# A graph-attention kernel: q rows in two PSUM banks per batch, q in a rounded and a rest part, tile sums per pair

## The chip, the cores and the metric

One core of a Trainium2 chip runs the kernel. It has TensorE (matmuls into PSUM), VectorE, ScalarE, GpSimd (which here issues the gathers by row index) and SyncE (which issues the other DMAs), and 16 DMA engines. The metric is device microseconds of one execution, lower is better.

## The reference

One layer of graph attention over 6250 nodes and 100000 edges, with edges sorted by destination, C = 256 channels in H = 8 heads of 32, all in float32:

```python
q, k, v = x @ Wq.T + bq, x @ Wk.T + bk, x @ Wv.T + bv       # each [6250, 8, 32]
score = clip(einsum("ehd,ehd->eh", q[dst], k[src]) / sqrt(32), -10, 10)
alpha = exp(score - max over the edges of a destination), divided by its sum
wv = segment_sum(alpha * v[src], dst)                       # [6250, 256]
y = x + wv @ Wp.T + bp
y = y + gelu(layernorm(y) @ W1.T + b1) @ W2.T + b2          # hidden 1024
out = layernorm(x + y)
```

## The kernel before

**Rows of k and v.** A first phase (to about 82 us) projects x into k and v for 25 units of 256 nodes with f32r matmuls on parts (a rounded part and a rest, `split_matmul`, L834), adds biases on VectorE and stores rows of k and v side by side in DRAM (`kv_rows`, 2 KB a row). The q rows of the first two units (`EARLY_Q`) are made there too; those of the other 24 are made one unit a turn later (`project_q` on TensorE, `copy_q` L1183 on ScalarE, `store_q_unit` on SyncE) and lie in `q_rows`, 1 KB a row.

**Edges.** The main phase walks over the edges in 196 batches of 4 tiles of 128 edges. Two batches are a pair, eight a turn; the index of a batch within the turn is i. As edges are sorted by destination, the 8 tiles of a pair need few q rows: SyncE loads four windows of 32 rows of q per pair into `qwin`, one per 32 partitions (`load_q_windows`, L597), two pairs ahead. For batch n:

- GpSimd gathers the k and v rows of the edges' sources, four indirect DMAs of 128 rows (L394), into one of 8 slots of `kv`. It may overwrite a slot when `ev` of batch n-8 is done (`s_ev`). A few tiles (one a turn) are instead projected from x by TensorE and copied by ScalarE.
- ScalarE makes the transposed one-hots `onehotT` (L1145, L1150), VectorE the upright ones `onehot` (L1550), per pair.
- TensorE multiplies one-hots with window rows into `quad`, four PSUM banks, 256 of each bank's 512 columns for one tile (`q_rows`, L895). Since the four banks hold one batch only, `q_rows(n+1)` waits for product n (`s_prod`).
- VectorE: `prod` = k times q rows (L1564), `score` = reduce over 32 (L1571), clip (L1578).
- ScalarE: exponent, once into PSUM bank 5 and once into `ev` (L1159, L1160).
- VectorE: `ev` = v times exponent (L1584). 
- TensorE: sums of the tiles into bank 4, each tile's nodes in a window of 32 partitions (`sums`, L904). The two batches of a pair accumulate.
- Per pair: ScalarE copies bank 4 (`stage`, L1168), TensorE merges the windows (`merge`, L884), ScalarE copies the merged sums into `acc_sb` (`copy_sums`, L1174), SyncE stores them (`store_sums`, L633). The next pair's sums write the same bank and wait for that copy (`s_accc`).

**Nodes.** Interleaved by hand, `node_steps(turn, i)` on each engine works on a unit of 256 nodes whose sums are complete: divide, transpose, project (L427), residual (L433), layer norm (VectorE root steps, L491 to L503), the feed-forward layers (`ffn1` L455 with ScalarE's bias L463, gelu, `ffn2` L475) and the output.

**Order.** Each engine has its program order written out in its own `edges` function, and waits on semaphores only. Before the change, iteration n of the four engines is:

```
TensorE: q_rows(n+1), merge of the pair two back (even n), node steps, sums(n-2)
VectorE: clip(n-1), product(n), onehots (even n), weight(n-2), node steps, scores(n)
ScalarE: exponent(n-1), copy_sums (even n), node steps, stage (odd n), transposed one-hots (even n)
GpSimd:  wait for ev of batch n-8, four gathers
```

`exists(...)` guards the ends. With i = 5 the node steps of TensorE stand behind the sums. `early_q` in the change is a view of `ev` that the first phase uses. There is a second, general path for inputs that the windows don't fit; it isn't run with these inputs.

## Time and profile before

| | us |
|---|---|
| median of 3 runs | 1517.91 |
| lowest and highest | 1514.08, 1532.04 |
| the profiled execution's own time | 1529.23 |
| its span, first to last instruction | 1527.4 |

The profile is one execution. Its page lists busy time by engine, the groups of instructions by line, DMA issues and the chain that ended last. Busy time of TensorE is the union of its matmuls, whose ends are modelled; a record of TensorE says when a matmul started, not when its signal arrived. An f32 matmul appears as two records, an f32r one as one. "x8" in a timeline row means that eight records follow each other without a gap. The bracket at a row's end is the idle time of that engine before it and what ended it; "remote" stands where the view finds no instruction that ended the wait, "issue" where the wait ended with no semaphore seen. The mean granted TensorE clock of this execution is 0.850 of full speed.

### The profile page before, as it was taken

How to read it: one execution, taken by the hardware profiler on the slowest of the kernel's cores; microseconds unless marked ns; L12 is line 12 of the kernel's file. 1: busy time of each engine (PE TensorE's matmuls, PEld its weight loads, DVE VectorE, ACT ScalarE, POOL GpSimd, SP SyncE). 2: the span in 40 equal slices, each digit the busy share in tenths (PEclk: the TensorE clock that was granted, in tenths of full speed). 3: DMA queues.
4: the chain of work that ended last, by engine and by line, in shares of the span. 5: the costliest groups of instructions: out<-in, count | busy, mean ns of one | idle time of the engine just before them, and what ended most of it. 6: DMA issues, size and time to landing. Idle time of an engine off the chain costs nothing.

```text
span 1527.4 us, 25002 instructions
## 1 busy us (share of the span) xinstructions
PE 1155.0 (76%) x6166; PEld 702.7 (46%) x6166; DVE 948.5 (62%) x1542; ACT 661.5 (43%) x1906; POOL 750.8 (49%) x800
## 2 busy tenths in 40 slices
PE   8946758768778588777678778677877876878887
PEld 6812325435444344444445444344444444545466
DVE  6816665666656565666666567576576665665673
ACT  2212225345445345345445435444545444534543
POOL 3664554545645544544555555545455545554300
PEclk9966868988978888979889888889788788898799
DMA  9975765655756656666666666756666656666510
GB/s 296 356 232 161 225 208 177 212 172 180 227 157 187 205 173 192 192 183 192 207 181 195 209 177 204 217 166 205 203 184 203 196 168 200 196 201 182 167 52 23
DMA packets 155028, 292.71 MB, mean 192 GB/s; under 512 B 32215, under 2 KB 92469, under 8 KB 154934
## 3 DMA queue, kind: packets, MB, share of 16 engines
q0 software_dynamic: 61536, 200.85, 43.6%
q1 hardware_dynamic: 93398, 90.90, 19.1%
q14 instruction: 72, 0.59, 0.1%
q8 instruction: 22, 0.36, 0.1%
HBM read 257.31 MB, written 34.34 MB: 191 GB/s over the span
## 4 chain that ended last, share of the span: by engine, by line
PE 32%; another core or an unknown queue 25%; issue 18%; DVE 18%; ACT 5%; DVEq 1%; ACTq 0%; DMA 0%; SPq 0%
DVE score L1571 7%; DVE ev L1584 6%; PE bank L475 5%; PE quad L834 4%; PE bank L455 4%; PE quad L895 4%; PE bank L904 4%; PE bank L427 2%; PE bank L917 2%; DVE prod L1564 2%; PE bank L930 1%; PE bank L884 1%; PE bank L421 1%; PE quad L455 1%
## 5 line engine op out<-in xcount | busy, mean ns | idle before, releaser
L394 POOL DMA_INDIRECT kv<-kv_rows,src_sb x750 | 713.7, 952 | 652.1 <-issue 326.4
L1564 DVE TENSOR_TENSOR prod<-kv,quad 128x1024 f32<-128x1024 f32 x196 | 239.3, 1221 | 426.3 <-remote 324.5
L904 PE MATMUL bank<-ev,onehot 128*32 128x264 f32 x1568 | 151.8, 451 | 160.7 <-ACT acc_sb L1174 101.4
L455 PE MATMUL bank<-hT,w_sb 128*128 128x256 f32 x736 | 219.2, 450 | 41.2 <-ACT hid L463 30.0
L1584 DVE TENSOR_TENSOR ev<-kv,bank 128x1024 f32<-128x1024 f32 x196 | 238.0, 1214 | 0.5 <-ACT ev L1160 0.5
L1571 DVE TENSOR_REDUCE score<-prod 128x32 f32<-128x1024 f32 x196 | 237.7, 1213 | 0.8
L895 PE MATMUL quad<-qwin,onehotT 32*128 32x256 f32 x1568 | 158.3, 476 | 79.1 <-issue 40.1
L455 PEld LDWEIGHTS bank<-hT,w_sb 128*128 128x128 f32 x736 | 162.8, 227 | 89.8 <-issue 45.4
L475 PE MATMUL bank<-w_sb,hid 128*128 128x256 f32 x736 | 190.9, 412 | 2.0 <-issue 2.0
L475 PEld LDWEIGHTS bank<-w_sb,hid 128*128 128x128 f32 x736 | 149.5, 208 | 32.0 <-issue 9.7
L1174 ACT ACTIVATE acc_sb<-bank 128x264 f32<-128x264 f32 x98 | 38.1, 389 | 290.7 <-remote 219.8
L463 ACT ACTIVATE hid<-bank,b_sb 128x256 f32<-128x256 f32 x184 | 77.1, 471 | 177.2 <-PE bank L455 76.0
L895 PEld LDWEIGHTS quad<-qwin,onehotT 32*128 32x128 f32 x1568 | 69.2, 205 | 181.5 <-issue 131.3
L904 PEld LDWEIGHTS bank<-ev,onehot 128*32 128x32 f32 x1568 | 35.5, 115 | 232.9 <-issue 206.5
L884 PE MATMUL bank<-staged,place 128*128 128x264 f32 x196 | 77.4, 480 | 54.6 <-ACT staged L1168 27.7
L930 PE MATMUL bank<-wqkv_in,xgT 128*128 128x512 f32 x120 | 80.7, 800 | 6.4 <-issue 6.1
L1159 ACT ACTIVATE bank<-clipped 128x32 f32<-128x32 f32 x196 | 38.4, 196 | 108.1 <-issue 75.9
L1168 ACT ACTIVATE staged<-bank 128x264 f32<-128x264 f32 x98 | 37.9, 387 | 84.6 <-remote 47.5
L884 PEld LDWEIGHTS bank<-staged,place 128*128 128x128 f32 x196 | 31.7, 203 | 92.2 <-issue 52.6
L421 PE MATMUL bank<-bias_rows,one_rows 2*128 2x512 f32 (+1 forms) x130 | 66.7, 513 | 8.9 <-issue 4.1
L427 PE MATMUL bank<-wp_sb,wvT 128*128 128x256 f32 x200 | 68.5, 502 | 0.0
L834 PE MATMUL quad<-wqkv_sb,xT_parts 128*128 128x512 f32 x288 | 67.2, 395 | 0.0
(148 smaller groups left out, 1297.7 us busy)
## 6 DMA issues: line engine op xcount, KB each, us to landing
dst_rows<-edge_dstT SPq DMA_DIRECT2D x50, 256.0 KB
qwin<-q_rows SPq DMA_DIRECT2D x392, 32.0 KB
kv_rows<-kv_out SPq DMA_DIRECT2D x24, 512.0 KB
kv<-kv_rows,src_sb POOLq DMA_INDIRECT x750
agg_rows<-acc_sb SPq DMA_DIRECT2D x98, 82.5 KB
xT_sb<-xT SPq DMA_DIRECT2D x25, 256.0 KB
xq_sb<-xT SPq DMA_DIRECT2D x25, 256.0 KB
agg_in<-agg_rows SPq DMA_DIRECT2D x24, 264.0 KB
```

The costliest lines, as they stand in the source:

```text
L394: return nc.gpsimd.indirect_dma_start(out=rows, out_offset=None, in_=kv_dram, in_offset=bass.IndirectOffsetOnAxis(ap=index, axis=0))
L427: last = nc.tensor.matmul(bank6[:, a * C:(a + 1) * C], wvT[:, (a * KC + k) * P:(a * KC + k + 1) * P], wp_sb[:, k * C:(k + 1) * C], start=F ...
L455: last = nc.tensor.matmul(bank[:, j * SB:(j + 1) * SB], w1_sb[:, k * HIDDEN + f * P:k * HIDDEN + (f + 1) * P], hT[:, k], start=(k == 0), s ...
L475: last = nc.tensor.matmul(bank[:, a * C:(a + 1) * C], hid[:, f, a * P:(a + 1) * P], w2_sb[:, f * C:(f + 1) * C], start=False, stop=(a == 1 ...
L834: last = nc.tensor.matmul(rows, lhsT, rhs, start=(n == 0), stop=(n == len(passes) - 1))
L884: nc.tensor.matmul(bank4[:, 0:ACC], place[:, slot % 2], staged[:, slot % 2], start=True, stop=True)\
L895: last = nc.tensor.matmul(quad[:, i, 0:C], onehotT[rows, slot // 2, cols], qwin[rows, slot // 2], start=True, stop=True)
L904: last = nc.tensor.matmul(bank4[WIN * i:WIN * (i + 1), 0:ACC], onehot[:, slot // 2, TILES * (slot % 2) + i, :], ev[:, slot % 4, i], start= ...
L930: last = nc.tensor.matmul(bank[:], columns[:, j], wqkv_in[:, j, C:3 * C], start=False, stop=(j == KC - 1))
L1564: nc.vector.tensor_tensor(prod[:, slot % 2].rearrange("p (i c) -> p i c", c=C), kv[:, slot, :, 0:C], quad[:, :, 0:C], ALU.mult).then_inc(s ...
L1571: nc.vector.tensor_reduce(score[:, slot % 2], prod[:, slot % 2].rearrange("p (h d) -> p h d", d=HD), AX.X, ALU.add).then_inc(s_score, 1)
L1584: nc.vector.tensor_tensor(ev[:, slot % 4, :, 0:C].rearrange("p i (h d) -> p i h d", d=HD), kv[:, slot, :, C:2 * C].rearrange("p i (h d) -> ...
```

## The change

- `q_rows` in DRAM has rows of 2 KB: the q row rounded to f32r, and the rest (q minus the rounded part). ScalarE's copy writes the rounded part, a new subtraction on VectorE the rest: `q_low` once a turn at i = 3, and one per early unit in the first phase (where the unrounded q is kept in `early_q`). Stores of q units become two DMAs. `qwin` and `onehotT` are f32r, `qwin` has both parts.
- `q_rows(n)` writes two whole banks: tiles 2i and 2i+1 of a pair share window i and bank i, so batch n uses banks 0 and 1 (even) or 2 and 3 (odd). Each tile takes two f32r matmuls that accumulate, rounded part and rest: eight matmuls of 256 columns, two windows at a time. It waits for product n-2, and TensorE's iteration n issues `q_rows(n+2)`. `q_rows(1)` moves into the opening.
- `sums` runs once per pair, in odd iterations, for all eight tiles; `s_part` counts pairs.
- `acc_sb` and `prod` lose half of their buffers (4 to 2, 2 to 1); the SBUF goes to `qwin`.
- The tiles of a pair are taken in their natural order; the tables of the host follow.

The diff, cut to its core ("..." marks what is left out: the general path, waits that count 32 instead of 16, the check's tables):

```diff
-    q_dram = nc.dram_tensor("q_rows", [Q_UNITS * SB, C], f32).ap()
+    q_dram = nc.dram_tensor("q_rows", [Q_UNITS * SB, 2 * C], f32).ap()
...
-        q_next = sb("q_next", [P, 2, C])
+        q_next = sb("q_next", [P, 2, 2, C], f32r)
...
-        onehotT = sb("onehotT", [P, 4, 2 * P])
+        onehotT = sb("onehotT", [P, 4, 2 * P], f32r)
         onehot = sb("onehot", [P, 4, PAIR_TILES, WIN])
-        qwin = sb("qwin", [P, 4, C])
+        qwin = sb("qwin", [P, 4, 2, C], f32r)
         ev = sb("ev", [P, 4, TILES, ACC])
-        acc_sb = sb("acc_sb", [P, 4, ACC])
+        acc_sb = sb("acc_sb", [P, 2, ACC])
...
-        prod = sb("prod", [P, 2, TILES * C])
+        prod = sb("prod", [P, TILES * C])
...
+        early_q = ev[:].rearrange("p a i n -> p (a i n)")[:, 0:EARLY_Q * 6 * C].rearrange("p (u t n) -> p u t n", u=EARLY_Q, t=3)
...
-                if u < EARLY_Q:
-                    sp.wait_ge(s_qb, u + 1)
-                    sp.dma_start(q_dram[u * SB:(u + 1) * SB, :].rearrange("(a p) n -> p a n", p=P), q_out[:, u])\
-                        .then_inc(s_qst, 16)
+                for e in range(EARLY_Q):
+                    if u == min(e + 2, UNITS - 1):
+                        sp.wait_ge(s_qlo, e + 1)
+                        for t in range(2):
+                            sp.dma_start(q_unit_rows(slice(e * SB, (e + 1) * SB))[:, t], early_q[:, e, t].rearrange("p (a n) -> p a n", n=C))\
+                                .then_inc(s_qst, 16)
...
-                    sp.dma_start(qwin[WIN * i:WIN * (i + 1), slot], q_dram[bass.ds(base + WINDOW_STARTS[i], WIN), :])\
-                        .then_inc(s_qwin[slot], 16)
+                    sp.dma_start(qwin[WIN * i:WIN * (i + 1), slot].rearrange("p t n -> p (t n)").bitcast(f32),
+                                 q_dram[bass.ds(base + WINDOW_STARTS[i], WIN), :]).then_inc(s_qwin[slot], 16)
...
             def store_q_unit(turn):
-                sp.wait_ge(f_qb, turn + 1)
+                sp.wait_ge(f_ql, turn + 1)
                 sp.sem_inc(s_gate_sp, 1)
-                sp.dma_start(q_dram[bass.ds((turn + EARLY_Q) * SB, SB), :].rearrange("(a p) n -> p a n", p=P), q_next[:])\
-                    .then_inc(f_qst, 16)
+                for t in range(2):
+                    sp.dma_start(q_unit_rows(bass.ds((turn + EARLY_Q) * SB, SB))[:, t], q_next[:, t].bitcast(f32))\
+                        .then_inc(f_qst, 16)
...
             def q_rows(n, slot, p, uses):
                 pe.wait_ge(s_qwin[slot // 2], 64 * uses)
                 pe.wait_ge(s_ohT, p + 1)
-                if exists(n - 1, BATCHES):
-                    pe.wait_ge(s_prod, n)
-                cols = slice(slot % 2 * P, (slot % 2 + 1) * P)
-                for i in range(TILES):
-                    rows = slice(WIN * i, WIN * (i + 1))
-                    last = nc.tensor.matmul(quad[:, i, 0:C], onehotT[rows, slot // 2, cols], qwin[rows, slot // 2],
-                                            start=True, stop=True)
+                if exists(n - 2, BATCHES):
+                    pe.wait_ge(s_prod, n - 1)
+                for j in range(2):
+                    for part in range(2):
+                        for i in (slot % 2 * 2, slot % 2 * 2 + 1):
+                            rows = slice(WIN * i, WIN * (i + 1))
+                            last = nc.tensor.matmul(quad[:, i, j * C:(j + 1) * C],
+                                                    onehotT[rows, slot // 2, j * P:(j + 1) * P],
+                                                    qwin[rows, slot // 2, part], start=(part == 0), stop=(part == 1))
                 last.then_inc(s_qe, 1)
 
-            def sums(n, slot, p):
-                pe.wait_ge(s_ev, n + 1)
-                if slot % 2 == 0 and exists(p - 1, PAIRS):
+            def sums(p, slot):
+                pe.wait_ge(s_ev, 2 * p + 2)
+                if exists(p - 1, PAIRS):
                     pe.wait_ge(s_accc, p)
-                for i in range(TILES):
-                    last = nc.tensor.matmul(bank4[WIN * i:WIN * (i + 1), 0:ACC],
-                                            onehot[:, slot // 2, TILES * (slot % 2) + i, :], ev[:, slot % 4, i],
-                                            start=(slot % 2 == 0 and (i > 0 or not exists(p - 1, PAIRS))),
-                                            stop=(slot % 2 == 1), skip_group_check=(i == 0))
+                for j in range(2):
+                    for i in range(TILES):
+                        tile = 2 * i + j
+                        last = nc.tensor.matmul(bank4[WIN * i:WIN * (i + 1), 0:ACC], onehot[:, slot, tile, :],
+                                                ev[:, (2 * slot + tile // TILES) % 4, tile % TILES],
+                                                start=(j == 0 and (i > 0 or not exists(p - 1, PAIRS))),
+                                                stop=(j == 1), skip_group_check=(i == 0))
                 last.then_inc(s_part, 1)
...
                 project_x(2, xgT)
+                q_rows(1, 1, 0, 1)
...
-                    pe.wait_ge(f_qb, s + 2)
+                    pe.wait_ge(f_ql, s + 2)
...
-                    if exists(n + 1, BATCHES):
-                        q_rows(n + 1, (i + 1) % SLOTS, 4 * turn + (i + 1) // 2, turn + (i + 1) // SLOTS + 1)
+                    if exists(n + 2, BATCHES):
+                        q_rows(n + 2, (i + 2) % SLOTS, 4 * turn + (i + 2) // 2, turn + (i + 2) // SLOTS + 1)
                     if i % 2 == 0 and exists(4 * turn + i // 2 - 2, PAIRS):
                         merge(4 * turn + i // 2 - 2, (i // 2 + 2) % 4)
                     if i != 5:
                         node_steps(turn, i)
-                    if exists(n - 2, BATCHES):
-                        sums(n - 2, (i - 2) % SLOTS, 4 * turn + (i - 2) // 2)
+                    if i % 2 == 1 and exists(4 * turn + i // 2 - 1, PAIRS):
+                        sums(4 * turn + i // 2 - 1, (i // 2 + 3) % 4)
...
+                for e in range(EARLY_Q):
+                    if u == min(e + 2, UNITS - 1):
+                        act.wait_ge(s_qb, e + 1)
+                        nc.scalar.activation(early_q[:, e, 0].bitcast(f32r), early_q[:, e, 2], ACT.Copy).then_inc(s_qhi, 1)
...
-            def exponent(n, slot):
+            def exponent(n, slot, p):
                 act.wait_ge(s_clip, n + 1)
                 if exists(n - 1, BATCHES):
                     act.wait_ge(s_ev, n)
                 if exists(n - 4, BATCHES):
-                    act.wait_ge(s_part, n - 3)
+                    act.wait_ge(s_part, p - 1)
                 first = EX_COL + slot % 2 * TILES * H
                 nc.scalar.activation(bank5[:, first:first + TILES * H], clipped[:, slot % 2], ACT.Exp, scale=SCALE)
                 nc.scalar.activation(ev[:, slot % 4, :, C:ACC],
...
                                      ACT.Exp, scale=SCALE).then_inc(s_exp, 1)
 
             def stage(p, slot):
-                act.wait_ge(s_part, 2 * p + 2)
+                act.wait_ge(s_part, p + 1)
                 if exists(p - 2, PAIRS):
                     act.wait_ge(s_mrg, p - 1)
                 nc.scalar.activation(staged[:, slot % 2], bank4[:, 0:ACC], ACT.Copy).then_inc(s_stc, 1)
 
             def copy_sums(p, slot):
                 act.wait_ge(s_mrg, p + 1)
-                if exists(p - 4, PAIRS):
-                    act.wait_ge(s_aggst, 16 * (p - 3))
-                nc.scalar.activation(acc_sb[:, slot], bank4[:, 0:ACC], ACT.Copy).then_inc(s_accc, 1)
+                if exists(p - 2, PAIRS):
+                    act.wait_ge(s_aggst, 16 * (p - 1))
+                nc.scalar.activation(acc_sb[:, slot % 2], bank4[:, 0:ACC], ACT.Copy).then_inc(s_accc, 1)
...
             def copy_q(turn):
                 act.wait_ge(f_qm, turn + 1)
                 if exists(turn - 1, Q_UNITS - EARLY_Q):
-                    act.wait_ge(f_qst, 16 * turn)
-                nc.scalar.activation(q_next[:].rearrange("p a c -> p (a c)"), bank6[:], ACT.Copy).then_inc(f_qb, 1)
+                    act.wait_ge(f_qst, 32 * turn)
+                nc.scalar.activation(q_next[:, 0].rearrange("p a c -> p (a c)"), bank6[:], ACT.Copy).then_inc(f_qb, 1)
...
+                for e in range(EARLY_Q):
+                    if u == min(e + 2, UNITS - 1):
+                        dve.wait_ge(s_qhi, e + 1)
+                        nc.vector.tensor_tensor(early_q[:, e, 1].bitcast(f32r), early_q[:, e, 2], early_q[:, e, 0],
+                                                ALU.subtract).then_inc(s_qlo, 1)
...
-                    dve.wait_ge(s_part, 2 * p - 6)
+                    dve.wait_ge(s_part, p - 3)
...
-                if exists(n - 2, BATCHES):
-                    dve.wait_ge(s_score, n - 1)
-                nc.vector.tensor_tensor(prod[:, slot % 2].rearrange("p (i c) -> p i c", c=C), kv[:, slot, :, 0:C],
-                                        quad[:, :, 0:C], ALU.mult).then_inc(s_prod, 1)
+                if exists(n - 1, BATCHES):
+                    dve.wait_ge(s_score, n)
+                nc.vector.tensor_tensor(prod[:].rearrange("p (i c) -> p i c", c=C), kv[:, slot, :, 0:C],
+                                        quad[:, slot % 2 * 2:slot % 2 * 2 + 2]
+                                        .rearrange("p b (j c) -> p (b j) c", c=C), ALU.mult).then_inc(s_prod, 1)
 
             def scores(n, slot):
                 dve.wait_ge(s_prod, n + 1)
                 if exists(n - 2, BATCHES):
                     dve.wait_ge(s_clip, n - 1)
-                nc.vector.tensor_reduce(score[:, slot % 2], prod[:, slot % 2].rearrange("p (h d) -> p h d", d=HD),
+                nc.vector.tensor_reduce(score[:, slot % 2], prod[:].rearrange("p (h d) -> p h d", d=HD),
...
+            def q_low(turn):
+                dve.wait_ge(f_qb, turn + 1)
+                nc.vector.tensor_tensor(q_next[:, 1].rearrange("p a c -> p (a c)"), bank6[:],
+                                        q_next[:, 0].rearrange("p a c -> p (a c)").bitcast(f32),
+                                        ALU.subtract).then_inc(f_ql, 1)
...
                 if i == 1 and exists(turn - 2, SUPERBLOCKS):
                     residual_twice(turn - 2)
+                if i == 3 and exists(turn, Q_UNITS - EARLY_Q):
+                    q_low(turn)
...
-    order = np.arange(EDGE_COLS).reshape(PAIRS, TILES, 2).transpose(0, 2, 1).reshape(-1)
-    tiles_dst = dst.reshape(EDGE_COLS, P)[order]
-    rows_dst = np.full((TURNS * SLOTS, TILES, P), NO_NODE, dst.dtype)
-    rows_dst[:BATCHES] = tiles_dst.reshape(BATCHES, TILES, P)
+    tiles_dst = dst.reshape(EDGE_COLS, P)
+    rows_dst = np.full((TURNS * HALF_TURN, TILES, 2 * P), NO_NODE, dst.dtype)
+    rows_dst[:PAIRS] = dst.reshape(PAIRS, TILES, 2 * P)
```

## Rows read from the trace of the kernel before

**Rows 1.** The page, part 1: busy time, share of the span, instructions.
```profile
PE 1155.0 (76%) x6166; PEld 702.7 (46%) x6166; DVE 948.5 (62%) x1542; ACT 661.5 (43%) x1906; POOL 750.8 (49%) x800
```

**Rows 2.** Busy time by stretch: us, busy (x instructions), TensorE clock, DMA share, GB/s.
```profile
12.00:82.30 70.30, 67.95 (x313) 56.14 (x311) 58.82 (x117) 18.59 (x30) 34.22 (x32) 1.00 0.99 339
...
100.00:1400.00 1300.00, 964.61 (x5263) 566.48 (x5263) 807.48 (x1238) 582.70 (x1722) 676.69 (x711) 0.84 0.64 192
```

**Rows 3.** Groups by line: line engine op | busy us, mean ns | idle before us <-releasers.
```profile
L394 POOL DMA_INDIRECT kv<-kv_rows,src_sb x750 | 713.7, 952 | 652.1 <-issue 326.4 <-DVE ev L1584 319.3 <-DMA kv_rows<-kv_out 6.5
L1564 DVE TENSOR_TENSOR prod<-kv,quad 128x1024 f32<-128x1024 f32 x196 | 239.3, 1221 | 426.3 <-remote 324.5 <-issue 56.2 <-PE quad L895 26.3
L1584 DVE TENSOR_TENSOR ev<-kv,bank 128x1024 f32<-128x1024 f32 x196 | 238.0, 1214 | 0.5 <-ACT ev L1160 0.5
...
L904 PE MATMUL bank<-ev,onehot 128*32 128x264 f32 x1568 | 151.8, 451 | 160.7 <-ACT acc_sb L1174 101.4 <-issue 57.9 <-DVE ev L1584 0.9
...
L1174 ACT ACTIVATE acc_sb<-bank 128x264 f32<-128x264 f32 x98 | 38.1, 389 | 290.7 <-remote 219.8 <-PE bank L884 61.2 <-issue 9.7
...
L1399 DVE TENSOR_TENSOR xT_parts<-xT_sb,xT_parts 128x512 fp32r<-128x512 f32 x25 | 17.3, 692 | 3.8 <-ACT xT_parts L1124 3.3
```

**Rows 4.** Timeline, 782 to 799 us, all engines: start us, us, instruction [idle before].
```profile
781.55 0.95 POOL L394 DMA_INDIRECT kv<-kv_rows,src_sb  x1 [1.74 <-issue]
...
782.65 0.66 PE L904 MATMUL bank<-ev,onehot 128*32 128x264 f32 x8
...
783.59 0.71 PE L895 MATMUL quad<-qwin,onehotT 32*128 32x256 f32 x8 [0.28 <-DVE prod L1564]
...
784.23 0.71 PE L884 MATMUL bank<-staged,place 128*128 128x264 f32 x2
...
786.53 5.05 SPq L597 DMA_DIRECT2D qwin<-q_rows  x4
...
786.64 0.17 DVE L1578 TENSOR_SCALAR clipped<-score 128x32 f32<-128x32 f32 x1
...
790.30 0.95 POOL L394 DMA_INDIRECT kv<-kv_rows,src_sb  x1 [0.30 <-issue]
791.62 1.22 DVE L1564 TENSOR_TENSOR prod<-kv,quad 128x1024 f32<-128x1024 f32 x1 [4.81 <-remote]
...
793.15 0.39 ACT L1174 ACTIVATE acc_sb<-bank 128x264 f32<-128x264 f32 x1 [7.69 <-remote]
...
793.68 1.11 PE L904 MATMUL bank<-ev,onehot 128*32 128x264 f32 x8 [7.01 <-ACT acc_sb L1174]
...
794.72 1.24 PE L895 MATMUL quad<-qwin,onehotT 32*128 32x256 f32 x8
794.76 0.94 POOL L394 DMA_INDIRECT kv<-kv_rows,src_sb  x1 [3.51 <-DVE ev L1584]
...
795.40 0.21 ACT L1160 ACTIVATE ev<-clipped 128x32 f32<-128x32 f32 x1
...
796.89 1.22 DVE L1564 TENSOR_TENSOR prod<-kv,quad 128x1024 f32<-128x1024 f32 x1 [0.97 <-PE quad L895]
```

**Rows 5.** Timeline of VectorE after that, 799 to 806 us: the next late product.
```profile
805.37 1.22 DVE L1564 TENSOR_TENSOR prod<-kv,quad 128x1024 f32<-128x1024 f32 x1 [4.45 <-remote]
```

**Rows 6.** Timeline of the opening, 93 to 121 us, all engines.
```profile
97.50 0.68 PE L923 MATMUL bank<-ident,hid 128*128 128x128 f32 x2 [3.41 <-issue]
...
115.13 0.95 POOL L394 DMA_INDIRECT kv<-kv_rows,src_sb  x1 [0.30 <-issue]
...
120.70 0.38 ACT L1196 ACTIVATE xgT<-bank 128x256 f32<-128x256 f32 x1 [23.26 <-remote]
```

**Rows 7.** The gathers of L394 alone: ns min/median/max, first and last start us.
```profile
L394 POOL DMA_INDIRECT kv<-kv_rows,src_sb x750: 940/946/1297, 82.6 to 1441.0; - x188
```

**Rows 8.** Timeline of TensorE, 12.2 to 13.5 us: f32r matmuls of 256 columns.
```profile
11.83 1.65 PE L834 MATMUL bank<-wqkv_sb,xT_parts 128*128 128x256 f32 x11
```

**Rows 9.** DMA issues by tile: queue, count, KB each.
```profile
qwin<-q_rows SPq DMA_DIRECT2D x392, 32.0 KB
```

67 lines of the change are left out of this document (34 added, 33 removed).

## The prediction, made before the result was known

> **What bounds the kernel now.** I read the page's busy shares first, then the groups by line, then two stretches of the timeline. No engine fills the span: TensorE 76%, VectorE 62%, ScalarE 43%, GpSimd 49% [rows 1]. From 100 to 1400 us VectorE is busy 807 of 1300 us [rows 2], though every batch passes through it. The groups say what it waits for: the product `prod` stands idle 426 us, of which 324.5 + 56.2 + 26.3 = 407 us end with "remote", "issue" and the q-row matmuls, the weighting `ev` 0.5 us; ScalarE's copy into `acc_sb` waits 290.7 us, 219.8 of it "remote" [rows 3].
>
> The timeline shows what the remote is. Eight q-row records start at 783.59 and end by 784.30, the merge ends at 784.94. The product that needs those q rows starts at 791.62, the copy that needs the merge at 793.15 [rows 4]. Between them GpSimd issues gathers, eight in a row from 781.55 to 791.25, 1.25 us each (0.95 and 0.30 idle). The product starts 0.4 us after the last, the copy 1.9 us after. The opening shows it larger: x transposes that ran at 97.50 are copied at 120.70, and the unbroken row of gathers ends at 116.08 [rows 6]. That copy waits for no gathered kv row, and in the steady part a gather stands eight batches ahead in the program. So I read it thus: a TensorE signal given some 3 us or more into a row of gathers reaches the others only when the row is over. This is inferred; no view names the cause.
>
> The kernel therefore turns in a cycle: the end of `ev` frees a slot, GpSimd issues the gathers (750 x 1.25 = 938 us in all [rows 3]), TensorE's signals are held, VectorE runs out of q rows, GpSimd runs dry, the signals come, and it starts again. Products at 791.62 and 805.37, two batches apart, span one cycle of 13.8 us [rows 4, 5]. GpSimd's gathers start between 82.6 and 1441.0 [rows 7]: 1358 - 938 = 420 us without them, or 4.3 us for each of 98 cycles of two batches.
>
> **The change part by part.**
> *q rows two batches ahead.* `q_rows(n+2)` is issued where `q_rows(n+1)` was, after product n. But `weight(n)` needs `exponent(n)`, which ScalarE runs only after it has left its iteration n, where it waits for the merge (even) or the tile sums (odd), both TensorE signals. That is late next. In the stretch shown, the clip of the batch before ends at 786.81 and the product could follow instead of at 791.62. VectorE would do that product, one weighting and the next product, and then stand before the weighting whose exponent ends at 795.61 [rows 4]. It now comes to that at 796.89 + 1.22 = 798.1: at best 2.5 us gained. But the first weighting, 4.8 us earlier, frees a slot while GpSimd is still issuing, so four gathers lengthen the row by 5.0 us, the merge is held 5.0 us longer, and the exponent ends at 800.6: 2.5 us lost. I take 0 for the first wait of a cycle. Other bounds: a third of the cycles falls away, 33 x 4.3 = -142 us; or the loss, the second rival.
> *Sums per pair.* Now the sums of an even batch wait for `acc_sb`, with the next q rows queued behind them: 101.4 us [rows 3]. In the stretch, sums start at 793.68, q rows at 794.72, and VectorE waits a second time, 0.97 us at 796.89 [rows 4]. Now those q rows stand ahead of the sums, which move to the odd iteration. Part of the 101 us lies while GpSimd still has gathers to issue and is worth nothing. I take half, -50 us; bounds 0 and -101. Against it, both batches' sums lie directly ahead of `stage`: 0.66 us more (eight records at 782.65), at most 98 x 0.66 = 65 us. It passes while the signal is held anyway: 0.
> *Matmuls in f32r.* Before: four f32 matmuls, eight records in 0.71 us [rows 4]. After: eight f32r matmuls of 256 columns. The nearest row has eleven at 128 rows in 1.65 us [rows 8], so one each 0.14 us after a first of about 0.28. With two row tiles side by side a batch takes 3 x 0.14 + 0.28 = 0.7 us, with no overlap 7 x 0.14 + 0.28 = 1.3 us: 0 to +0.55 us on an engine that has usually finished when VectorE waits. I take 0 (bounds 0 and 196 x 0.55 = +108). The Trainium skill (TensorE: Matmul & The Clock Gate, Part 3) has matmuls in different 32-row groups run together; eight records in 0.71 us agree. By it the change gives up four-way packing for two-way, and the sum stays the 0.7 us above. The Trainium skill also says (TensorEngine Tiling (Array Packing), Key Properties) that changing the tiling mode drains the array; half as many blocks of sums means fewer changes, which no row here prices.
> *q in two parts.* Each of 24 turns gets a subtraction `q_low` on VectorE: 24 x 0.69 = 16.6 us by the split of the same size, L1399 [rows 3]. It waits for ScalarE's `copy_q`, itself behind the held merge; queued behind it are normalise, the scores of its batch and the next product, for which GpSimd and TensorE then wait. In the cycle shown ScalarE resumes 1.5 us after VectorE; always met, 24 x 1.5 = 36 us. I take 8: +25 us in all (bounds 0 and +53). The early units' two splits lie under projections that fill TensorE for 68.0 of 70.3 us [rows 2]: 0, otherwise 2 x 0.69 and two ScalarE copies, under 3 us.
> *Queues and DMA.* 392 q loads of 32 KB become 64 KB [rows 9], and each turn's store of q rows becomes two. DMA engines are 64% busy [rows 2], loads are asked two pairs ahead: 0. SyncE issues one DMA more a turn, ahead of `load_q_unit`; at the slow 5.05 us for four [rows 4] that is 24 x 1.3 = 31 us if exposed, but it feeds things needed a turn later: 0. Two `acc_sb` buffers instead of four: the store two pairs back is two cycles old, 0. One `prod` buffer: the clip already waits for that reduce, 0. The order of tiles costs nothing.
>
> **Sum.** 1527.4 - 50 + 25 = 1502 us of span. The profiled execution's own time is 1529.2, so 1504 of it, a ratio of 0.984. It ran 0.7% over the median shown, and 1517.9 x 0.984 = 1493 us.
>
> **Rivals.**
> *Three batches per cycle.* ScalarE's exponent is in time, because signals given early in a row of gathers do pass: the q rows at 794.72, with the row starting at 794.76, serve the product at 796.89 [rows 4]. Then 33 cycles fall away: 1529.2 - 142 + 17 = 1404, on the median 1394 us. For it: all of VectorE's idle time sits before the product and 0.5 us before `ev`. Against it: `ev` is never late only because the product is.
> *Slower: the exponent sets the restart.* Now a restart begins with the product and the weighting follows 1.14 us later. If it waits for the exponent, ScalarE first does what stands between 793.15 and 795.61, 2.46 us: 1.3 us more in each such cycle, 129 us in 98. With +25 and -50 this passes 2% (31 us) once 43% of the cycles show it; at 60% it is 77 + 25 - 50 = +52, or 1569 us.
> *The change does not touch the bound.* If the product waits for gathered rows after all, the 16.6 us of q_low remain: 1534 us. The x transposes of [rows 6] speak against it.
>
> **How the numbers follow.** Forecast 0.42, three batches 0.30, slower restart 0.18, untouched 0.10. A measurement of this kernel tells about 2% from no change: 1488 and 1548 us. The forecast's own bounds (-101 with 0, 0 with +53) are 1418 and 1570; I put 0.11 of its 0.42 under 1488 and 0.02 over 1548. Faster 0.30 + 0.11 = 0.41; slower 0.14 of the second rival + 0.02 = 0.16; same 0.43. The 8-in-10 range runs from 1385, just under the three-batch case, to 1560, cutting off less than half of each outer case.
>
> **What would show it.** Right: most of the 407 us before `prod` go and idle time appears before `ev`, `onehot` and `q_low`; ScalarE keeps its "remote" waits; the sums' wait for `acc_sb` falls under 30 us; GpSimd's time without gathers stays near 400 us. Three batches: rows of twelve gathers, 280 us without them. Slower: over 1.5 us idle before `ev` or `q_low` in most cycles. Wrong altogether: `prod` still waits 300 us with its q rows long done, outside any row of gathers. Least sure is how far into a row of gathers a signal still passes.

## The result, and the profile after

| | before | after |
|---|---|---|
| median, us | 1517.37 (1514.08 to 1532.04) | 1570.07 (1557.65 to 1578.63) |
| the profiled execution's own time | 1529.23 | 1557.65 |
| its span | 1527.4 | 1555.8 |

The ratio is 1.032, with an interval of 1.024 to 1.041: the change makes the kernel slower. Here and below a ratio leaves out executions that took over 1.5% longer than the fastest of the same kernel. The range (1385 to 1560) missed it by 10 us, and slower had been given 0.16.

The page of the kernel after, part 1, the same stretch as in [rows 2], and its gathers alone:

```profile
PE 1152.2 (74%) x6166; PEld 773.7 (50%) x6166; DVE 971.4 (62%) x1565; ACT 659.8 (42%) x1908; POOL 750.6 (48%) x800
```
```profile
100.00:1400.00 1300.00, 938.80 (x5104) 617.82 (x5105) 807.68 (x1223) 560.86 (x1673) 661.74 (x697) 0.81 0.66 201
```
```profile
L401 POOL DMA_INDIRECT kv<-kv_rows,src_sb x750: 943/949/1407, 83.3 to 1468.6; - x188
```

No engine is fuller than before. VectorE is busy 22.9 us longer than in [rows 1] (971.4 - 948.5), of which 16.6 are `q_low`. Its idle time is 584.4 us (1555.8 - 971.4) against 578.9: 5.5 us more. So the long waits before the product went, and others of the same size came. The gathers take as long as before each, but the last starts 27.6 us later than in [rows 7]. The groups by line of the kernel after show where the waits now are (busy us, mean ns, idle before and what ended it), first VectorE, then TensorE, then ScalarE:

```profile
L1585 DVE TENSOR_TENSOR prod<-kv,quad 128x1024 f32<-128x1024 f32 x196 | 239.2, 1220 | 160.1 <-remote 76.2 <-ACT kv L1224 56.3 <-issue 20.8
L1606 DVE TENSOR_TENSOR ev<-kv,bank 128x1024 f32<-128x1024 f32 x196 | 238.4, 1216 | 154.1 <-ACT ev L1180 116.6 <-issue 37.6
...
L1571 DVE TENSOR_TENSOR onehot<-dloc,bank 128x256 f32<-128x256 f32 x98 | 40.9, 417 | 79.0 <-ACT ev L1180 69.7 <-issue 8.7 <-PE bank L918 0.4
...
L1614 DVE TENSOR_TENSOR q_next<-bank,q_next 128x512 fp32r<-128x512 f32 x24 | 16.6, 692 | 21.0 <-ACT q_next L1203 14.8 <-issue 6.3
```
```profile
L906 PE MATMUL quad<-qwin,onehotT 32*128 32x256 f32 x1568 | 158.2, 322 | 43.3 <-issue 31.1 <-DVE prod L1585 12.2
L918 PE MATMUL bank<-ev,onehot 128*32 128x264 f32 x1568 | 113.8, 405 | 2.6 <-issue 2.6
L894 PE MATMUL bank<-staged,place 128*128 128x264 f32 x196 | 85.9, 526 | 159.9 <-ACT staged L1188 81.6 <-issue 78.3
...
L1194 ACT ACTIVATE acc_sb<-bank 128x264 f32<-128x264 f32 x98 | 38.3, 391 | 239.3 <-remote 145.4 <-PE bank L894 67.1 <-issue 26.6
L1188 ACT ACTIVATE staged<-bank 128x264 f32<-128x264 f32 x98 | 38.3, 390 | 238.8 <-remote 204.4 <-PE bank L918 27.2 <-issue 7.0
```

Two rows of the kernel before stand beside them, in the same view:

```profile
L884 PE MATMUL bank<-staged,place 128*128 128x264 f32 x196 | 77.4, 480 | 54.6 <-ACT staged L1168 27.7 <-issue 26.7
...
L1168 ACT ACTIVATE staged<-bank 128x264 f32<-128x264 f32 x98 | 37.9, 387 | 84.6 <-remote 47.5 <-PE bank L904 25.2 <-issue 11.8
```

The product's idle time fell from 426 us [rows 3] to 160, and 154 us came before the weighting, 79 before the one-hots. Of the 160 us, 56 end with a copy by ScalarE (`kv` L1224, a tile projected from x); before, 15.9 us did. The sums' wait for `acc_sb` fell from 101 us to nothing, while the merge's wait, mostly for `staged`, rose from 55 to 160 us. ScalarE's two copies together waited 375 us before (290.7 + 84.6) and 478 after.

One cycle of the kernel after (timeline, 782 to 796 us) shows how it goes. Its row of gathers starts at 780.35:

```profile
782.32 1.10 PE L918 MATMUL bank<-ev,onehot 128*32 128x264 f32 x16
...
783.35 0.76 PE L906 MATMUL quad<-qwin,onehotT 32*128 32x256 f32 x8
...
785.50 1.21 DVE L1585 TENSOR_TENSOR prod<-kv,quad 128x1024 f32<-128x1024 f32 x1
...
789.12 0.94 POOL L401 DMA_INDIRECT kv<-kv_rows,src_sb  x1 [0.30 <-issue]
791.00 0.39 ACT L1188 ACTIVATE staged<-bank 128x264 f32<-128x264 f32 x1 [8.31 <-remote]
...
791.70 0.21 ACT L1180 ACTIVATE ev<-clipped 128x32 f32<-128x32 f32 x1
791.94 1.22 DVE L1606 TENSOR_TENSOR ev<-kv,bank 128x1024 f32<-128x1024 f32 x1 [5.23 <-ACT ev L1180]
...
793.95 0.95 POOL L401 DMA_INDIRECT kv<-kv_rows,src_sb  x1 [3.88 <-DVE ev L1606]
```

VectorE has its q rows and starts the product at 785.50 without a wait. The tile sums ended at 783.42, the row of gathers at 790.06, and ScalarE copies those sums at 791.00. Its exponent stands behind that copy, VectorE's weighting behind the exponent, the next gathers behind the weighting.

Here the signal arrives after the row. In another cycle of the same trace it is late too, but arrives while GpSimd still issues gathers of the row that began at 551.99 (551 to 565 us):

```profile
551.99 0.95 POOL L401 DMA_INDIRECT kv<-kv_rows,src_sb  x1 [1.73 <-DVE ev L1606]
...
553.10 1.10 PE L918 MATMUL bank<-ev,onehot 128*32 128x264 f32 x16
...
559.09 0.39 ACT L1188 ACTIVATE staged<-bank 128x264 f32<-128x264 f32 x1 [5.57 <-remote]
...
564.57 0.95 POOL L401 DMA_INDIRECT kv<-kv_rows,src_sb  x1 [0.30 <-issue]
```

A row of gathers is here, and below, a run of gather records less than 0.6 us apart. Of the 50 "remote" waits of this copy, 19 end inside a row (73 of the 204 us); of the 72 before the product in the kernel before, also 19 (48 of 324.5 us). So a held signal comes late, most often after the row's end, but the end of the row isn't a fixed gate.

### The profile page after: what moved, and what is told of

It reads as the page before. It is cut to its first block, busy times and chain, and to the rows that moved or that the text cites. A ratio compares the mean times of both kernels' runs of the same rounds, so it can differ in the third digit from the quotient of the medians.

```text
span 1555.8 us, 25092 instructions
## 1 busy us (share of the span) xinstructions
PE 1152.2 (74%) x6166; PEld 773.7 (50%) x6166; DVE 971.4 (62%) x1565; ACT 659.8 (42%) x1908; POOL 750.6 (48%) x800
## 4 chain that ended last, share of the span: by engine, by line
PE 37%; another core or an unknown queue 25%; issue 17%; ACT 10%; DVE 9%; DMA 1%; ACTq 1%; SPq 0%; DVEq 0%
PE bank L462 9%; PE bank L482 4%; PE quad L844 3%; PE bank L918 3%; DVE score L1593 3%; PE bank L894 3%; PE quad L906 3%; PE bank L434 2%; PE bank L944 2%; DVE ev L1606 2%; PE bank L931 2%; PE bank L428 2%; ACT hid L470 1%; ACT y_out L514 1%
## 5 line engine op out<-in xcount | busy, mean ns | idle before, releaser
L462 PE MATMUL bank<-hT,w_sb 128*128 128x256 f32 x736 | 254.0, 506 | 135.1 <-ACT hid L470 112.8
L1585 DVE TENSOR_TENSOR prod<-kv,quad 128x1024 f32<-128x1024 f32 x196 | 239.2, 1220 | 160.1 <-remote 76.2
L1606 DVE TENSOR_TENSOR ev<-kv,bank 128x1024 f32<-128x1024 f32 x196 | 238.4, 1216 | 154.1 <-ACT ev L1180 116.6
L462 PEld LDWEIGHTS bank<-hT,w_sb 128*128 128x128 f32 x736 | 184.7, 257 | 181.3 <-ACT hid L470 101.3
L482 PE MATMUL bank<-w_sb,hid 128*128 128x256 f32 x736 | 199.1, 414 | 31.5 <-issue 31.2
L894 PE MATMUL bank<-staged,place 128*128 128x264 f32 x196 | 85.9, 526 | 159.9 <-ACT staged L1188 81.6
L906 PE MATMUL quad<-qwin,onehotT 32*128 32x256 f32 x1568 | 158.2, 322 | 43.3 <-issue 31.1
L906 PEld LDWEIGHTS quad<-qwin,onehotT 32*128 32x128 f32 x1568 | 116.3, 203 | 129.7 <-issue 113.7
L1188 ACT ACTIVATE staged<-bank 128x264 f32<-128x264 f32 x98 | 38.3, 390 | 238.8 <-remote 204.4
L918 PE MATMUL bank<-ev,onehot 128*32 128x264 f32 x1568 | 113.8, 405 | 2.6 <-issue 2.6
L1571 DVE TENSOR_TENSOR onehot<-dloc,bank 128x256 f32<-128x256 f32 x98 | 40.9, 417 | 79.0 <-ACT ev L1180 69.7
L944 PE MATMUL bank<-wqkv_in,xgT 128*128 128x512 f32 x120 | 67.8, 691 | 1.1 <-issue 1.1
L440 DVE TENSOR_TENSOR x<-bank,x_in 128x512 f32<-128x512 f32 x24 | 16.6, 692 | 81.8 <-remote 37.8
L918 PEld LDWEIGHTS bank<-ev,onehot 128*32 128x32 f32 x1568 | 42.5, 112 | 50.7 <-issue 30.4
```

The lines of the kernel that those rows point to most:

```text
L462: last = nc.tensor.matmul(bank[:, j * SB:(j + 1) * SB], w1_sb[:, k * HIDDEN + f * P:k * HIDDEN + (f + 1) * P], hT[:, k], start=(k == 0), s ...
L482: last = nc.tensor.matmul(bank[:, a * C:(a + 1) * C], hid[:, f, a * P:(a + 1) * P], w2_sb[:, f * C:(f + 1) * C], start=False, stop=(a == 1 ...
L894: nc.tensor.matmul(bank4[:, 0:ACC], place[:, slot % 2], staged[:, slot % 2], start=True, stop=True)\
L906: last = nc.tensor.matmul(quad[:, i, j * C:(j + 1) * C], onehotT[rows, slot // 2, j * P:(j + 1) * P], qwin[rows, slot // 2, part], start=( ...
L918: last = nc.tensor.matmul(bank4[WIN * i:WIN * (i + 1), 0:ACC], onehot[:, slot, tile, :], ev[:, (2 * slot + tile // TILES) % 4, tile % TILE ...
L944: last = nc.tensor.matmul(bank[:], columns[:, j], wqkv_in[:, j, C:3 * C], start=False, stop=(j == KC - 1))
```

## The experiments

The change has three parts, called here **A** (q rows two batches ahead, in two whole banks), **B** (sums per pair) and **C** (q in two parts, f32r). The experiments ran on five chips, and on those the kernel before had two very different times: 1094 us on three of them, 1516 and 1539 us on the other two. The result above is of the second sort. I call the slow sort holding chips, the other free chips; each ratio is to the kernel before on the same chip. No chip was visited twice, so the chip and the moment of the visit can't be told apart. The diffs below show the core of each edit ("..." marks what is left out).

| run | what | chip | ratio (95%) |
|---|---|---|---|
| r1_after | the change, A + B + C | free | 1.012 (1.009 to 1.016) |
| e1_unsplit | A + B | free | 1.014 (1.012 to 1.016) |
| e2_one_ahead | B + C | free | 1.014 (1.011 to 1.017) |
| e3, h3_sums_per_batch | A + C | free | 1.027 (1.025 to 1.029), 1.030 (1.028 to 1.032) |
| e4_stage_behind_exponent | A + B + C, ScalarE's order | free | 1.193 (1.189 to 1.197) |
| e5, e6 (plain loads) | before; after | free | 0.973 (0.969 to 0.976); 1.026 from two runs |
| h1, h2 (two by two) | before; after | free | 1.000 (0.999 to 1.001); 1.012 (1.008 to 1.016) |
| e9_before_sums_per_pair | B | holding | 1.023 (1.013 to 1.032) |
| g1_two_ahead_alone | A | holding | 1.069 (1.060 to 1.078) |
| g2_split_alone | C | holding | 1.007 (1.004 to 1.010) |
| g3_plain_before | before, plain loads | holding | 0.693 (0.688 to 0.697) |
| e7_pace_before | before, paced | holding | 0.959 (0.949 to 0.968) |
| e8_pace_after | after, paced | holding | 0.968 (0.960 to 0.976) |
| g4_per_batch_paced | A + C, paced | holding | 0.972 (0.966 to 0.978) |

### The parts, on free chips

e1_unsplit (q whole):

```diff
-                                                    qwin[rows, slot // 2, part], start=(part == 0), stop=(part == 1))
+                                                qwin[rows, slot // 2], start=True, stop=True)
...
```

> The changed kernel, but q is kept whole: 1 KB rows in DRAM, no subtraction per turn, and four f32 matmuls for a batch's q rows (each fills half of one of the batch's two banks). Two batches ahead and sums per pair stay. Theory H (the loss is that ScalarE's exponent stands in program order behind a copy that waits for a TensorE signal held back by a row of gathers, which reading q rows two ahead has uncovered): the slowdown stays, ratio to before 1.01 to 1.04, VectorE still idle over 150 us before its weighting and its one-hots. Rival F (the f32r matmuls, their weight loads, 774 us instead of 703, and the subtraction cost the time): 1.00 or less.

e2_one_ahead:

```diff
-                    pe.wait_ge(s_prod, n - 1)
+                    pe.wait_ge(s_prod, n)
...
-                        q_rows(n + 2, (i + 2) % SLOTS, 4 * turn + (i + 2) // 2, turn + (i + 2) // SLOTS + 1)
+                        q_rows(n + 1, (i + 1) % SLOTS, 4 * turn + (i + 1) // 2, turn + (i + 1) // SLOTS + 1)
```

> The changed kernel, but the q rows of batch n+1 are made after product n, as before; q in two parts and sums per pair stay. Theory H: the exponent is covered again by the late product, so idle time before the weighting falls from 154 us to under 20 and that before the product goes back over 300; ratio 0.97 to 1.01. Rival F: 1.02 to 1.04. Rival P (sums per pair, whose 16 records now stand directly ahead of the copy into staged, cost the time): 1.02 to 1.04.

e3_sums_per_batch:

```diff
-                    for i in range(TILES):
+                    for i in (slot % 2 * 2, slot % 2 * 2 + 1):
...
-                    if i % 2 == 1 and exists(4 * turn + i // 2 - 1, PAIRS):
-                        sums(4 * turn + i // 2 - 1, (i // 2 + 3) % 4)
+                    if exists(n - 2, BATCHES):
+                        sums(n - 2, (i - 2) % SLOTS, 4 * turn + (i - 2) // 2)
```

> The changed kernel, but the tile sums of each batch are issued one iteration apart, as before (the new order of tiles stays). Theory H: little changes, 1.02 to 1.05. Rival P: ScalarE's remote wait ahead of staged falls from 204 us towards the 47 of before, ratio 1.00 or less. Rival F: 1.02 to 1.04.

The kernel before took 1093.9 us there, so none of the three could tell what I had asked. r2_before and r1_after (both kernels unchanged) say what is different:

> The kernel before, for its trace on this chip. Where it takes about 1094 us: one row of some 700 gathers without a pause, TensorE over 90% busy, idle time before the product under 60 us. Where it takes about 1517 us, the trace of before again, 426 us idle before the product.

> The changed kernel once more, because the first four experiments found another chip: the kernel before took 1094 us there, not 1517, and TensorE's signals arrived within 0.4 us also in rows of gathers. Theory H says that the slowdown of 3.2% comes from held signals. Where the kernel before takes about 1094 us the change then costs no more than its own work: 1.00 to 1.03, with idle time before weighting and one-hots under 20 us. Where it takes about 1517 us, 1.02 to 1.05 and 230 us of such idle time. Rival W (the change is slower by its own extra work on TensorE): about 1.03 on either.

r2_before took 1093.4 us. Its page, the row of its gathers, the product's group, and its opening:

```profile
PE 1004.7 (92%) x6166; PEld 629.5 (58%) x6166; DVE 946.8 (87%) x1542; ACT 658.3 (60%) x1906; POOL 749.8 (69%) x800
```
```profile
L394 POOL DMA_INDIRECT kv<-kv_rows,src_sb x750: 941/949/1470, 82.3 to 1022.4; - x188
```
```profile
L1564 DVE TENSOR_TENSOR prod<-kv,quad 128x1024 f32<-128x1024 f32 x196 | 239.1, 1220 | 59.5 <-DMA kv<-kv_rows,src_sb 42.4
```
```profile
99.86 0.95 POOL L394 DMA_INDIRECT kv<-kv_rows,src_sb  x1 [0.30 <-issue]
...
99.97 0.44 PE L923 MATMUL bank<-ident,hid 128*128 128x128 f32 x2
...
100.44 0.39 ACT L1196 ACTIVATE xgT<-bank 128x256 f32<-128x256 f32 x1 [0.37 <-PE bank L923]
```

The busy times of VectorE, ScalarE and GpSimd and the length of a gather are those of the holding chip. TensorE is busy 150 us less than in [rows 1] (1004.7 against 1155.0) at a granted clock of 0.979 instead of 0.850; busy time times clock is the same, 984 and 982 us. But the transposes of 99.97 are copied at 100.44, in the midst of an unbroken row of gathers, where [rows 6] has 97.50 and 120.70; no wait of this trace ends with "remote". GpSimd issues all 750 gathers in one row, 940 us, and that row is the bound. In r1_after the idle time before the weighting is 1.0 us. So the long waits are gone with the held signals, and the change still costs 1.2% there. Rival W falls (it expected about 3% on either sort), and so does rival F as the cause of all of the 3.2%. Rival P, the sums per pair ahead of the copy into `staged`, needs held signals and is not settled here; e9 below bears on it. A + C at 1.027 is not a clean removal of B: with the new order of tiles the sums of one batch lie in two windows instead of four, and eight records take TensorE 1.08 us instead of 0.65 (215 us busy in all, 111 with B).

### Are the gathers what holds the signals?

g3_plain_before, e5_plain_before (the same kernel) and e6_plain_after load other rows than the reference wants, in one instruction a batch. They leave out the gather by index, and read the same 4096 rows in every turn:

```diff
-                    for t in range(gathered(n) - len(x_tiles(turn, i))):
-                        col = (i % 4) * TILES + t
-                        gather_rows(kv[:, i, t, :], src_sb[:, buffer, col:col + 1]).then_inc(s_kv[i], 16)
+                    tiles = gathered(n) - len(x_tiles(turn, i))
+                    nc.gpsimd.dma_start(kv[:, i, 0:tiles, :], kv_dram[i * TILES * P:(i * TILES + tiles) * P, :]
+                                        .rearrange("(t p) n -> p t n", p=P)).then_inc(s_kv[i], 16)
```

> The kernel before, but GpSimd loads each batch with one plain DMA of 512 consecutive rows instead of four gathers by row index, so the same bytes come with a quarter of GpSimd's instructions, and other edges' rows (the gather by index is left out). Theory H, where the kernel before takes about 1517 us: rows of work on GpSimd are at most 2 us long, so signals pass and the time falls to 1050 to 1250 us; where it takes about 1094 us, little changes, 0.94 to 1.00. Rival D (not GpSimd's gathers but the DMA traffic or TensorE's clock holds the kernel back): at 1517 us it stays above 1400.

> The changed kernel with the same plain loads (the gather by index is left out). Theory H: its ratio to the kernel with plain loads and without the change is 0.99 to 1.03 on either chip, with under 30 us idle before the weighting. Rival S (reading q rows two ahead is slower in itself, with or without held signals): over 1.03, with idle time before the weighting as in the changed kernel.

> The kernel before with one plain DMA a batch in place of four gathers by index (the gather by index is left out), for a chip on which the kernel before takes about 1517 us: earlier it ran where that took 1094 us and gave 0.973. Theory H (rows of gather instructions hold TensorE's signals): 1050 to 1250 us, a ratio of 0.70 to 0.82. Rival D (the bytes moved, or the clock, hold the kernel at 1500 us): over 0.92.

On the holding chip the time fell from 1538.8 to 1065.5 us, what it is on a free chip (1063.3). The page of g3_plain_before, the stretch from 100 to 1000 us (same columns as [rows 2]) and its loads:

```profile
PE 997.5 (94%) x6166; PEld 627.1 (59%) x6166; DVE 947.8 (89%) x1542; ACT 655.6 (62%) x1906; POOL 184.6 (17%) x246
```
```profile
100.00:1000.00 900.00, 858.19 (x5541) 521.09 (x5533) 848.17 (x1301) 604.53 (x1808) 140.55 (x187) 0.99 0.86 287
```
```profile
L808 POOL DMA_DIRECT2D kv<-kv_rows x196: 741/748/807, 81.6 to 973.7; - x196
```

The DMA engines move more a second than before (287 GB/s against 192 in [rows 2]), TensorE does the same work (997.5 us at 0.985, again 983), no wait of the trace ends with "remote", and the 473 us are gone. So neither bytes nor TensorE's clock hold the kernel, the rows of gathers do. Whether it is their number or their being by index isn't separated: a plain load stands alone between waits, except for eight in the opening. Why a chip holds or doesn't is open.

e7_pace_before breaks the rows with the reference's rows kept:

```diff
                         pool.wait_ge(s_ev, n - SLOTS + 1)
+                        pool.wait_ge(s_part, n - SLOTS + 1)
```

> The kernel before; GpSimd waits ahead of the gathers of batch n not only for the weighting of batch n-8 but also for its tile sums, a TensorE signal. So no row of gathers is longer than four, and each ends until a TensorE signal has passed. Theory H, where the kernel before takes about 1517 us: the holes that its rows need anyway are bought back by signals that pass, 1250 to 1450 us. Where it takes about 1094 us, GpSimd's unbroken row of gathers is the bound there (720 of them without an idle moment but its own 0.30 us), and the wait only costs: 1.00 to 1.10. Rival: ratio 1.0 on either, because a slot is never waited for.

1452.4 us, 4.1% under the kernel before, 2 us above the range that was expected. Of rows of ten gathers or more the trace has one, the opening, against 8 in the trace before. The first line of VectorE's waits was 324.5 us [rows 3] and is now:

```profile
DVE prod L1565 <- remote: 185.1, 61, 23.0
```

e8_pace_after waits for q rows (`s_qe, n - SLOTS + 5`) instead, g4_per_batch_paced for the sums as e7 does.

> The changed kernel; GpSimd waits ahead of the gathers of batch n also for the q rows of batch n-4, the last that TensorE has made when the slot comes free. Theory H, where the kernel before takes about 1517 us: 1250 to 1500 us and the idle time before the weighting halved; where it takes about 1094 us: 1.01 to 1.08, as nothing is gained for the wait.

> The changed kernel with the tile sums of each batch in its own iteration, and GpSimd waiting ahead of the gathers of batch n also for the tile sums of batch n-8 (as in the kernel before with that wait, which had 0.959). Theory H: where the kernel before takes about 1517 us, 0.93 to 0.97; where it takes about 1094 us, 1.03 to 1.06, since the wait then only costs. Rival S: over 0.97 at 1517 us.

Both come to 0.97, no better than the kernel before with its wait: e8 still has 152.4 us idle before the weighting, where half of 154 was expected. With the same wait in both, A + C costs 1.3% (g4's 0.972 against e7's 0.959, two chips). Against the change itself e8 gains about 6% (0.968 / 1.032, two different chips).

### The parts, on holding chips

e9_before_sums_per_pair, B in the kernel before, where the order of tiles stays and the sums of a pair still lie in four windows:

```diff
-            def sums(n, slot, p):
-                pe.wait_ge(s_ev, n + 1)
+            def sums(p, slot):
+                pe.wait_ge(s_ev, 2 * p + 2)
...
-                    if exists(n - 2, BATCHES):
-                        sums(n - 2, (i - 2) % SLOTS, 4 * turn + (i - 2) // 2)
+                    if i % 2 == 1 and exists(4 * turn + i // 2 - 1, PAIRS):
+                        sums(4 * turn + i // 2 - 1, (i // 2 + 3) % 4)
```

> The kernel before with one part of the change alone: the tile sums of a pair are issued together in the odd iteration. The earlier four runs, where the kernel before took 1094 us, had 1.012 to 1.014 with sums per pair and 1.027 with sums per batch in the new kernel. Theory E (own work on a busy TensorE: fewer changes between kinds of matmul save time, so this part gains and the others cost): 0.98 to 1.00 at 1094 us. Rival: it delays the store of the sums and so VectorE's division: 1.00 to 1.02, with the wait for agg_in at over 15 us. Where the kernel before takes 1517 us: 0.95 to 1.00 by the prediction's second step.

It went the other way: 1546.8 us against 1515.7, 31 us or 2.3% slower. Groups of its VectorE, TensorE and ScalarE:

```profile
L1565 DVE TENSOR_TENSOR prod<-kv,quad 128x1024 f32<-128x1024 f32 x196 | 239.3, 1221 | 457.0 <-remote 318.7 <-ACT kv L1205 54.4 <-issue 51.9
...
L905 PE MATMUL bank<-ev,onehot 128*32 128x264 f32 x1568 | 114.5, 412 | 1.5 <-issue 0.7 <-DVE ev L1585 0.7
L884 PE MATMUL bank<-staged,place 128*128 128x264 f32 x196 | 89.1, 544 | 213.2 <-ACT staged L1169 116.8 <-issue 96.4
...
L1175 ACT ACTIVATE acc_sb<-bank 128x264 f32<-128x264 f32 x98 | 38.3, 390 | 198.4 <-remote 97.8 <-PE bank L884 69.3 <-issue 31.1
L1169 ACT ACTIVATE staged<-bank 128x264 f32<-128x264 f32 x98 | 38.0, 388 | 296.6 <-remote 256.8 <-PE bank L905 31.0 <-issue 8.8
```

The sums' wait is gone (160.7 us in [rows 3], 1.5 here), and as much came back one step on, ahead of the merge (54.6 to 213.2). Both batches' sums now give one signal, and the copy into `staged` waits for it with "remote" 256.8 us instead of 47.5.

Two cycles show why. In the kernel before, sums that start 1.10 us into a row of eight gathers (781.55 and 782.65 in [rows 4]) are copied at once; in e9 sums that start 1.10 us into a row of eight are copied 4.9 us after their end:

```profile
783.38 0.39 ACT L1168 ACTIVATE staged<-bank 128x264 f32<-128x264 f32 x1 [0.27 <-PE bank L904]
```
```profile
956.20 0.95 POOL L394 DMA_INDIRECT kv<-kv_rows,src_sb  x1 [1.78 <-DVE ev L1585]
...
957.30 1.10 PE L905 MATMUL bank<-ev,onehot 128*32 128x264 f32 x16
...
963.31 0.39 ACT L1169 ACTIVATE staged<-bank 128x264 f32<-128x264 f32 x1 [5.55 <-remote]
```

Sixteen records end 0.44 us later than eight, 2.2 us into the row instead of 1.8. Over the two traces, in rows of seven gathers or more: of sums that end 1.6 to 2.0 us into the row (17 in the kernel before, none in e9) each is copied within 1.1 us; of those that end at 2.0 to 2.6 us, 7 of 14 take 1.9 us or more before, and 19 of 21 take 1.8 us or more in e9. So sums per pair turned a signal that passed into one that is held.

The cost arrives at the product: its idle time is 457.0 us instead of 426.3, and these 31 us are the 31 us of the run. They don't come through the q rows: "remote", "issue" and the q-row matmuls together end 399 us of it, 407 before. ScalarE's copy of a projected tile ends 54.4 us instead of 15.9. It stands directly behind the copy into `acc_sb`, as in this cycle of e9 (782 to 786 us):

```profile
782.37 0.39 ACT L1169 ACTIVATE staged<-bank 128x264 f32<-128x264 f32 x1 [8.65 <-remote]
...
782.82 1.25 PE L884 MATMUL bank<-staged,place 128*128 128x264 f32 x2 [5.79 <-ACT staged L1169]
...
784.18 0.39 ACT L1175 ACTIVATE acc_sb<-bank 128x264 f32<-128x264 f32 x1 [1.18 <-PE bank L884]
...
784.56 0.59 ACT L1205 ACTIVATE kv<-bank 128x512 f32<-128x512 f32 x1
...
785.34 1.22 DVE L1565 TENSOR_TENSOR prod<-kv,quad 128x1024 f32<-128x1024 f32 x1 [7.60 <-ACT kv L1205]
```

g1_two_ahead_alone is e1 and e3 together (A), g2_split_alone e2 and e3 (C). Both keep the new banks, the new order of tiles and the smaller buffers.

> Reading two batches ahead alone: the new banks and order of tiles, but q whole with four f32 matmuls a batch, and the tile sums of each batch in its own iteration. Theory H with the cause now put on the sums per pair: where the kernel before takes about 1517 us, 0.98 to 1.01 (the exponent is late next, so the q rows in time gain nothing); where it takes about 1094 us, 1.00 to 1.03. Rival S (the two-ahead reading is what slows the change): 1.02 to 1.04 at 1517 us, with over 150 us idle before the weighting.

> q in two parts with f32r matmuls alone: the q rows are made one batch ahead as before, the sums per batch. Where the kernel before takes about 1517 us, theory H with the sums as cause expects 1.00 to 1.02 (q_low 8 to 25 us and its place on VectorE); rival F (split, its weight loads and its DMA bytes cost the 3.2%): 1.02 to 1.04. Where it takes about 1094 us the DMA engines are at 88%, and 20 MB more put them at 95%: 1.01 to 1.03.

C with the two-window sums costs 0.7%. A with them costs 6.9%, more than either theory had expected. Groups of VectorE and TensorE in g1 (the profile is of the slowest of its four runs, 1677 of 1641 to 1677 us):

```profile
L1592 DVE TENSOR_TENSOR ev<-kv,bank 128x1024 f32<-128x1024 f32 x196 | 238.4, 1216 | 237.7 <-ACT ev L1171 190.8 <-issue 46.9
```
```profile
L902 PE MATMUL quad<-qwin,onehotT 32*128 32x256 f32 x1568 | 240.4, 428 | 23.9 <-DVE prod L1571 21.9 <-issue 2.0
L914 PE MATMUL bank<-ev,onehot 128*32 128x264 f32 x1568 | 237.3, 428 | 119.3 <-ACT acc_sb L1185 82.3 <-issue 35.3 <-DVE ev L1592 1.6
```

The wait for the exponent is A's: before the weighting 237.7 us here and 154.1 in the change, 0.5 in e9 and in g2, which read one ahead. But g1 also gives TensorE 82 us more of q rows (240.4 against 158.3: whole f32 matmuls with two row groups instead of four) and 86 us more of sums, so its 6.9% is not A's alone. h3 was to tell the two apart and found a free chip.

> The changed kernel with the tile sums of each batch in its own iteration, as run before where the kernel before took 1094 us (1.027 there). Where it takes 1510 to 1540 us: two ahead alone gave 1.069 with q whole and q in two parts alone 1.007. If two ahead costs the 6% itself, 1.05 to 1.08 here, and sums per pair give back 3% beside it though they cost 2.3% alone. If the 6% came from the four whole f32 matmuls in the new banks, 1.00 to 1.03.

Beside B, A and C together add 0.9% (1.032 against 1.023, on two chips, with overlapping intervals). No run takes B alone out of the change on a holding chip, so how the 3.2% divides between A and B inside the change is open: B alone is enough for most of it, and A alone would be enough for more than all.

### Two that change an order

e4_stage_behind_exponent:

```diff
                     if i % 2 == 0 and exists(done, PAIRS):
+                        stage(done, (i // 2 + 2) % 4)
+                    if i % 2 == 1 and exists(done, PAIRS):
                         copy_sums(done, (i // 2 + 2) % 4)
...
-                    if i % 2 == 1 and exists(done + 1, PAIRS):
-                        stage(done + 1, (i // 2 + 3) % 4)
```

> The changed kernel with ScalarE's program reordered alone: the copy into staged goes from the end of the odd iteration to behind the exponent of the even one, the copy into acc_sb behind the exponent of the odd one, so that both waits for TensorE stand right behind an exponent instead of ahead of one. Theory H: the exponent is in time more often; idle time before weighting and one-hots falls from 233 us to under 100, ratio to before 0.94 to 1.00. Rivals F and P: no gain over the changed kernel, 1.02 to 1.05. If the sums are delayed by the later merge instead, it could end above 1.04, and TensorE's own waits for staged and acc_sb would show it.

1302.6 us. The exponent is in time, as expected (2.7 us before the weighting), but the sums are stored an iteration later, and VectorE's division waits for them in each of the 24 turns (waits of VectorE: us, times, longest):

```profile
DVE den L406 <- DMA agg_in<-agg_rows: 104.8, 24, 6.8
DVE x L440 <- PE bank L434: 62.0, 24, 4.6
```

In r1_after the first of these is 17.7 us in 10 waits, in r2_before 6.7 in 2. Whether the order helps on a holding chip wasn't tried.

h1_two_by_two_before and h2_two_by_two_after:

```diff
+                        if t == 2 and exists(n - SLOTS, BATCHES):
+                            pool.wait_ge(s_prod, n - SLOTS + 4)
+                            pool.sem_inc(s_gate_pool, 1)
```

> The kernel before; GpSimd waits between the second and the third gather of batch n for the product of batch n-5, which itself waits for TensorE's q rows. So a row of gathers can't grow while VectorE waits for TensorE. Theory H, where the kernel before takes 1510 to 1540 us: rows of two to six gathers, 1300 to 1440 us (0.85 to 0.95), idle time before the product under 200 us. Where it takes about 1094 us: 1.00 to 1.08. Rival: more and shorter rows hold the signals as long, ratio 0.96 or more at 1510 to 1540 us.

> The changed kernel with the same wait between second and third gather. There the q rows of two batches lie ready, so VectorE's product seldom waits for TensorE and the wait breaks a row less surely. Theory H: 0.90 to 0.99 where the kernel before takes 1510 to 1540 us, slower than the same wait in the kernel before; 1.01 to 1.08 where it takes about 1094 us. Rival S: 1.0 or more, since ScalarE's copies are what waits.

On the free chip the wait costs nothing (1.000, and 1.012 like the change without it). What it does on a holding chip is open.

### The cost on free chips

The change costs 1.2% where nothing is held. The stretch from 400 to 700 us of r2_before, then of r1_after:

```profile
400.00:700.00 300.00, 283.04 (x1828) 173.97 (x1827) 275.82 (x427) 206.22 (x614) 227.11 (x240) 1.00 0.88 282
```
```profile
400.00:700.00 300.00, 276.99 (x1818) 188.60 (x1820) 280.40 (x427) 201.95 (x600) 227.39 (x239) 1.00 0.94 297
```

GpSimd's row is the bound in both (227 us), so most of the added VectorE work is hidden, and the DMA engines go from 88 to 94%. With the row out of the way the cost shows: 1118.7 and 1124.9 us in e6's two faster runs (the others took 1138.5 and 1139.0) against 1063.3 in e5, 5.5%. That is outside what theory H had expected (0.99 to 1.03) and inside rival S's figure, but the idle time before the weighting is 6.9 us, not S's. In e6 VectorE waits 25.7 us for `agg_in`, and TensorE's granted clock is 0.957 over the span where e5 has 0.985; the rest of the 59 us I can't name.

## Why the prediction was wrong, point by point

- **What bounds the kernel**: right in the main. Rows of gathers hold TensorE's signals. It had been inferred; the plain loads show it (0.693 on a holding chip, 0.973 on a free one), and so does the opening of r2_before. The rule beside it, free up to some 3 us and then held until the row is over, was too simple: sums that end at 2.2 us are held already, and a quarter of the "remote" waits before the product end inside a row. The 420 us without gathers were the size of the effect: 1517 us less 1094 on a free chip is 423. That one kernel has both times, by chip or by visit, was not foreseen.
- **q rows two batches ahead, taken as 0**: the mechanism was right, the size is open. Of the 407 us before the product 97 remain (76.2 + 20.8) besides 3.3 that end with the q-row matmuls, and the exponent was late next. Beside B, A and C add 0.9%, so the 0 may stand there; alone A costs up to 6.9% (106 us), part of it TensorE's own work. The step had 0, with the second rival's 129 us as its upper bound. Rows of ten or more gathers went from 8 to 18, as the step had said of four gathers added to a row.
- **Sums per pair, taken as -50**: this is the step that failed. The wait for `acc_sb` fell to nothing, as foreseen, but alone the part costs 2.3%, about 35 us of 1518. I priced the wait that goes, and took the longer block of sums ahead of `stage` as 0 since it "passes while the signal is held anyway". In most pairs the signal had not been held: e9's block of sums is 0.44 us longer, and the "remote" waits of `staged` go from 16 to 45, from 47.5 to 256.8 us. Behind it wait the merge, the copy into `acc_sb`, ScalarE's copy of the projected tile and so the product (31 us more). Shown in the kernel before; inside the change the `staged` wait is 204.4 us, and its price there wasn't measured.
- **f32r matmuls, taken as 0**: right. Eight records take 0.74 to 0.76 us in most batches, where 0.7 was estimated, and TensorE's q-row time is the same (158.2 against 158.3). By the Trainium skill (TensorE: Matmul & The Clock Gate, Part 3) matmuls in different row groups of the array run together; the trace agrees where the groups are halved for whole f32 matmuls, 1.13 us instead of 0.71 in g1.
- **q in two parts, taken as +25**: 16.6 us of work and 21.0 of waits in the profile. C alone gave +0.7%, about 11 us. Queues: the DMA engines are 66% busy on the holding chip and 94% on a free one; no run prices the queues by themselves.
- **The rivals**: the slower one named the right place. Idle time before the weighting and the one-hots is 233 us, 2.4 us for each of 98 cycles. That its 1569 us stands beside 1570 is luck, owed to two errors: it took -50 for B, and with +35 there it would give 1655, so its price for the restart was too high. The forecast's own terms with B at +35 come to 1517.9 + 25 + 35 = 1578 us, 8 from the result; no run shows that these terms add. Three batches per cycle came now and then: 17 rows of eleven or twelve gathers against 6 before, among some 130 rows. But the time without gathers rose to 447 us (1468.6 - 83.3 - 938), where that rival had 280.
- **The signs**: every sign named for "right" came, the long wait before the product gone, idle time before `ev`, `onehot` and `q_low`, the sums' wait under 30 us, and the time still went the other way. They tested which wait goes, not what the next one costs.

I had given the slower case 0.18; it needed 43% of the cycles. In the trace VectorE stops 83 times, 47 before the weighting and 36 before the one-hots, for 98 pairs; 41 and 22 of these stops are longer than 1.5 us.

## What to carry to other kernels

When a wait on a late signal is removed, list every other consumer of that producer's signals and ask which now waits in its place; merging two signals into the later one can make a wait of it (0.44 us did here). If a stall ends without a visible releaser, swap the suspected instruction for one that moves the same bytes with fewer issues: one such run decided more here than seven that undid parts of the change. And read the unchanged kernel's time beside every comparison, as its bound may be another on the next chip or visit.

## What the runs showed of the hardware

The same kernel took 1091 to 1096 us on three chips and 1500 to 1550 on others, each visited once, with equal busy times of VectorE, ScalarE and GpSimd and equal 0.95 us gathers. On the latter a TensorE signal given while GpSimd issues a row of indirect DMAs can reach ScalarE and VectorE late: 22.5 us after the end of the transposes in the opening (98.18 to 120.70), 7.6 us in the cycle shown above (783.42 to 791.00), 4.9 us with the row still running (554.20 to 559.09). On the former it is there within 0.1 us of the matmuls' end, inside a row of 750 (100.41 to 100.44).

When a signal is held isn't a matter of the row's end alone. In rows of seven gathers or more, sums that end 1.6 to 2.0 us into the row were copied within 1.1 us (17 of 17 in the kernel before; the one in the kernel after was held for 6.5 us), later ones mostly not (19 of 21 at 2.0 to 2.6 us in e9). Yet in the opening of the kernel before, whose row starts at 82.62, matmuls that end at 90.58 are copied at 90.62. What fills or empties in between no run shows.

With plain DMAs of 1 MB from the same queue, 0.75 us each, no wait ends with "remote" on either sort of chip; a long row of them was not tried. The granted clock follows (0.85 and 0.98 over the span): the low clock is an effect of the waits, as the plain loads on a holding chip bring 0.985.
